# Second expert stage's entry: choice on exponentials, first expert's weights spread by TensorE from the token-major table, two more steps' passes made ahead

## What is computed

```
scores = softmax(x @ gate_w.T)                      # 8 experts, in 4 groups of 2
the 2 groups with the largest scores stay; of their experts the 2 largest are chosen
topk_w = topk_w / topk_w.sum(-1)                    # weights of the two, summing to 1
combine = zeros(T, 8) with the weights at the chosen experts
gate, up = x @ w13[e]  (256 columns each)
out = sum over e of (silu(gate) * up * combine[:, e]) @ w2[e]
```

## Time and profile before

| | |
|---|---|
| median of 3 runs | 1080.58 us |
| profiled execution, time and span | 1081.86 us, 1080.1 us |
| PE busy | 1018.0 us, 94% |
| DVE busy | 817.6 us, 76% |
| ACT busy | 791.2 us, 73% |
| POOL busy | 232.2 us, 21% |
| 16 DMA engines, mean | 176 GB/s |
| chain that ended last | PE 85%; DVE 6%; ACT 3%; POOL 2%; DMA 2%; issue 2% |

### The profile page before, as it was taken

How to read it: one execution, slowest core, us unless ns; L and a number is a source line. 1 busy time by engine, 2 the same in 40 slices (tenths; PEclk the granted TensorE clock), 3 DMA queues, 4 the chain that set the end, 5 groups by cost and what they waited for, 6 DMA issues and landing times.

```text
span 1080.1 us, 20283 instructions
## 1 busy us (share of the span) xinstructions
PE 1018.0 (94%) x5216; PEld 689.6 (64%) x5248; DVE 817.6 (76%) x1867; ACT 791.2 (73%) x1323; POOL 232.2 (21%) x355
## 2 busy tenths in 40 slices
PE   5799999999987799999999999999998998899996
PEld 3233333333345488888888888888875776788884
DVE  8544444444448499999999999999986888589997
ACT  6699999999964587777788777788774443455554
POOL 3777764455452000000000000000014113100000
PEclk9999999999988999999999999999999998899999
DMA  4478786667750587777777777777720000224231
GB/s 137 130 234 261 243 260 229 215 221 235 226 178 1 181 290 238 242 241 242 241 240 241 239 238 243 241 243 243 241 85 25 1 1 1 62 88 136 93 112 40
DMA packets 103422, 190.54 MB, mean 176 GB/s; under 512 B 11980, under 2 KB 56652, under 8 KB 103372
## 3 DMA queue, kind: packets, MB, share of 16 engines
q1 hardware_dynamic: 103380, 190.06, 54.2%
HBM read 154.03 MB, written 35.98 MB: 176 GB/s over the span
## 4 chain that ended last, share of the span: by engine, by line
PE 85%; DVE 6%; ACT 3%; POOL 2%; DMA 2%; issue 2%; SPq 0%; DVEq 0%; POOLq 0%; ACTq 0%
PE bank L1381 27%; PE bank L1394 16%; PE bank L1236 11%; PE bank L1388 8%; PE bank L1217 6%; PE bank L1220 5%; PE bank L1483 2%; PE bank L1247 1%; PE bank L1467 1%; POOL m_norm L831 1%; PE bank L1122 1%; DMA ring<-c_rows 1%; ACT silu_z L1062 1%; DVE xn L1591 1%; PE bank L1486 1%
## 5 line engine op out<-in xcount | busy, mean ns | idle before, releaser
L1381 PE MATMUL bank<-xh,w_parts 128*128 128x512 f32 x896 | 278.3, 392 | 1.6 <-DVEq L1807 1.6
L948 ACT ACTIVATE ring<-bank,minus_bound 128x1024 f32<-128x1024 f32 x256 | 262.6, 1122 | 9.4 <-DVE bank L1688 6.5
L1036 ACT ACTIVATE bank<-bank 128x512 f32<-128x512 f32 x320 | 186.2, 582 | 89.1 <-PE bank L1381 89.1
L1821 DVE TENSOR_TENSOR bank<-bank,ring 128x512 f32<-128x512 f32 x320 | 223.9, 700 | 27.7 <-DMA ring<-c_rows 3.3
L1394 PE MATMUL bank<-hh,w_parts 128*128 128x512 f32 x776 | 239.4, 390 | 0.0
L1813 DVE TENSOR_TENSOR hl<-bank,hh 128x512 fp32r<-128x512 f32 x321 | 218.6, 681 | 0.1
L1030 ACT ACTIVATE hh<-bank 128x512 fp32r<-128x512 f32 x321 | 190.6, 594 | 3.0 <-DVE bank L1821 2.9
L1381 PEld LDWEIGHTS bank<-xh,w_parts 128*128 128x128 f32 x896 | 168.4, 189 | 38.0 <-DVEq L1807 1.8
L1688 DVE TENSOR_TENSOR bank<-bank,corner 128x128 f32<-128x128 f32 x256 | 76.4, 299 | 150.9 <-PE bank L1220 148.5
L1381 PE MATMUL bank<-xl,w_parts 128*128 128x512 f32 x448 | 175.3, 391 | 0.0
L1394 PEld LDWEIGHTS bank<-hh,w_parts 128*128 128x128 f32 x776 | 145.9, 188 | 30.6 <-ACT hh L1030 0.4
(11 more groups left out here) (310 smaller groups left out, 1138.5 us busy)
## 6 DMA issues: line engine op xcount, KB each, us to landing
ring<-c_rows SPq DMA_DIRECT2D x176, 512.0 KB, 4.8
w_parts<-w_pairs SPq DMA_DIRECT2D x160, 128.0 KB, 3.3
w_pairs<-xh SPq DMA_DIRECT2D x16, 768.0 KB, 4.4
q_stack<-q_parts SPq DMA_DIRECT2D x64, 144.0 KB
k_stack<-k_parts SPq DMA_DIRECT2D x192, 48.0 KB
w_pairs<-xl SPq DMA_DIRECT2D x16, 512.0 KB, 3.0
big<-in_w_exp SPq DMA_DIRECT2D x16, 384.0 KB, 4.8
w_ffn_parts<-xl SPq DMA_DIRECT2D x16, 384.0 KB, 3.9
```

The lines of the kernel that those rows point to most:

```text
L948: act.activation(ring[:, c % RING * S:(c % RING + 1) * S], wide[(m + c) % SB][:], ACT.Exp, bias=minus_bound[:]).then_inc(exp_done, 1)
L1036: act.activation(bank(4 + c % ZB), bank(4 + c % ZB), ACT.Silu).then_inc(silu_ready, 1)
L1381: ins = pe.matmul(out_, w[i], x_[j], start=start and k == 0, stop=stop and k == 2, skip_group_check=not start)
L1821: dve.tensor_tensor(bank(4 + c % ZB), bank(4 + c % ZB), cb[u][:, g * GW:(g + 1) * GW], ALU.mult).then_inc(hid_ready, 1)
```

## The change

- The choice works on the shifted logits; the exponentials go to a tile of their own (exp8) and are needed only where the chosen scores are compared. The division by the sum goes, since the weights are divided by their own sum anyway.
- The first expert's weights no longer come by DMA: PE multiplies each tile's column of combine2, read as 128 equal columns (`across`), with the identity, 16 products of 128x128 in plain f32; ACT copies the four banks to cb[0] and raises the semaphores that the DMA raised. The transposes for the other experts' rows follow, each half behind a wait for ACT's copies (cb_loaded), because they use banks 0 to 3 now. ACT makes both row copies. SP loads only expert 1's rows at this place.
- Gate and up of steps 0 and 1 (FT 1, groups 0 and 1) are made ahead, in banks 4 to 7, between FT 0 and the spreading; ACT's two Silus too. In the loop steps 0 and 1 then have no PE work; the products with zeros go, those that open the banks too: each bank is opened by its first high product. The first body of the loop is written out on PE, DVE and ACT.
- DVE's order in a step is now hid n, gated n+4, hl of n-1, in all steps.
- Spare products: 18 for 14 ahead of norm 3, four ahead of each of its later transpositions (L1119), 2 for 12 and 0 for 4 further on.

```diff
@@ -270,6 +270,7 @@
         place = choice(62, 1)
+        exp8 = choice(64, 8).rearrange("p (t e) -> p t e", t=NT)
         earlier = sb("earlier", [P, 4, 4])
@@ -630,8 +631,7 @@
             sp.wait_ge(c_saved, (2 * G + 1) * 16)
-            for u in range(2):
-                load_rows2(u, u)
+            load_rows2(1, 1)
             with sp.Fori(0, NE2 // 2 - 1) as i:
@@ -1074,7 +1074,7 @@
             act.wait_ge(shifted, 1)
-            act.activation(soft[:], soft[:], ACT.Exp).then_inc(exp2_ready, 1)
+            act.activation(exp8, soft[:], ACT.Exp).then_inc(exp2_ready, 1)
             high_x(G - 1)
@@ -1082,20 +1082,40 @@
                 act.activation(first_up[g], bank(2 * (g % 2) + 1), ACT.Copy).then_inc(first_taken, 1)
-            act.wait_ge(c2T_psum, 1)
-            act.activation(c2T[:, 0:S], wide[2][0:NE2, :], ACT.Copy).then_inc(c2T_ready, 1)
-            act.sem_inc(hh2_ready, CREDIT - 1)
+            for c in range(2):
+                ready(act, gate_z, G + c)
+                act.activation(act_out[c], bank(4 + 2 * c), ACT.Silu).then_inc(silu2_ready, 1)
+            for g in range(G):
+                act.wait_ge(c2T_psum, g + 1)
+                ins = act.activation(cb[0][:, g * GW:(g + 1) * GW], bank(g), ACT.Copy)
+                if g % 2:
+                    ins.then_inc(cb_loaded[g // 2], 16)
+            act.sem_inc(hh2_ready, CREDIT)
+
+            def take_c2T(h):
+
+                act.wait_ge(c2T_psum, G + h + 1)
+                act.activation(c2T[:, h * S:(h + 1) * S], wide[h][0:NE2, :], ACT.Copy).then_inc(c2T_ready, 1)
+
+            take_c2T(0)
...
                 n = i * (2 * G) + c
+                if isinstance(i, int) and n < 2:
+                    if n == 1:
+                        high_part(n, c, hid[0], hid2_ready, down2_done, hh2_ready)
+                        take_c2T(1)
+                    return
                 if not last or c < G:
...
-            with act.Fori(0, NE2 - 1) as i:
+            for c in range(2 * G):
+                ffn_step(0, c, False)
+            with act.Fori(1, NE2 - 1) as i:
                 for c in range(2 * G):
@@ -1387,11 +1407,12 @@
-            def down_high(done_step, w, n, ready_high):
+            def down_high(done_step, w, n, ready_high, opens=False):
...
                 ready(pe, ready_high, n)
-                for part in w:
-                    ins = pe.matmul(bank(done_step % G), part, hh[done_step % 2][:], start=False, stop=False, skip_group_check=True)
+                for k, part in enumerate(w):
+                    ins = pe.matmul(bank(done_step % G), part, hh[done_step % 2][:], start=opens and k == 0, stop=False,
+                                    skip_group_check=True)
                 return ins
@@ -1500,10 +1521,11 @@
-            spare(7, 14)
-            norm(3, router_logits2)
-            for opened in (gate_z, up_z, down2_done, low2_used):
-                pe.sem_inc(opened, CREDIT)
+            spare(7, 18)
+            pe.wait_ge(ffn_zero, 1)
+            norm(3, router_logits2, 4)
+            for opened, skipped in ((gate_z, 0), (up_z, 0), (down2_done, 2), (low2_used, 3)):
+                pe.sem_inc(opened, CREDIT + skipped)
             loaded2 = MT_N // CB * 32
@@ -1513,18 +1535,25 @@
                 three(bank(2 * (g % 2) + 1), ffn_parts(0, 1), (xh[:, cols], xl[:, cols]), True).then_inc(up_z, 1)
+            pe.wait_ge(shifted, 1)
+            pe.wait_ge(parts_loaded[CB - 1], loaded2 + 16)
+            for c in range(2):
+                cols = slice(c * GW, (c + 1) * GW)
+                three(bank(4 + 2 * c), ffn_parts(1, 0), (xh[:, cols], xl[:, cols]), True).then_inc(gate_z, 1)
+                three(bank(5 + 2 * c), ffn_parts(1, 1), (xh[:, cols], xl[:, cols]), True).then_inc(up_z, 1)
             pe.wait_ge(first_taken, G)
-            spare(0, 12)
+            spare(0, 2)
             pe.wait_ge(combine2_ready, 1)
-            for t in range(NT):
-                ins = pe.transpose(bank(4 + t // TPG)[0:NE2, t % TPG * P:(t % TPG + 1) * P], combine2[:, t, :], ident[:])
-            ins.then_inc(c2T_psum, 1)
-            spare(0, 4)
-            pe.wait_ge(ffn_zero, 1)
-            pe.wait_ge(c2T_ready, 2)
-            pe.wait_ge(parts_loaded[CB - 1], loaded2 + 16)
-            for g in range(G):
-                pe.matmul(bank(g), ffn_parts(CB - 1, 2)[0], hh[1][:], start=True, stop=False, skip_group_check=True)
+            for g in range(G):
+                for t in range(TPG):
+                    ins = pe.matmul(bank(g)[:, t * P:(t + 1) * P], across(combine2[:, g * TPG + t, 0:1], P), ident[:],
+                                    start=True, stop=True)
+                ins.then_inc(c2T_psum, 1)
+            for h in range(2):
+                pe.wait_ge(cb_loaded[h], MT_N // CB * 16 + 16)
+                for t in range(NT // 2):
+                    ins = pe.transpose(wide[h][0:NE2, t * P:(t + 1) * P], combine2[:, h * (NT // 2) + t, :], ident[:])
+                ins.then_inc(c2T_psum, 1)
@@ -1533,6 +1562,9 @@
                 n, u, g = i * turn_ + c, (c // G + 1) % CB, c % G
+                first = isinstance(i, int) and i == 0
+                if first and c < 2:
+                    return
                 cols = slice(g * GW, (g + 1) * GW)
@@ -1541,13 +1573,18 @@
                     three(bank(4 + 2 * (c % 2)), ffn_parts(u, 0), (xh[:, cols], xl[:, cols]), True).then_inc(gate_z, 1)
-                down_low(low, down2(low), n - 3, hl2_ready).then_inc(low2_used, 1)
+                if not first or c >= 3:
+                    down_low(low, down2(low), n - 3, hl2_ready).then_inc(low2_used, 1)
                 if ahead:
...
                     three(bank(5 + 2 * (c % 2)), ffn_parts(u, 1), (xh[:, cols], xl[:, cols]), True).then_inc(up_z, 1)
-                down_high(high, down2(high), n - 2, hh2_ready).then_inc(down2_done, 1)
-
-            with pe.Fori(0, FT_N // CB - 1) as i:
+                if first and c in (2, 4):
+                    pe.wait_ge(c2T_ready, c // 2)
+                down_high(high, down2(high), n - 2, hh2_ready, first and c < 2 + G).then_inc(down2_done, 1)
+
+            for c in range(turn_):
+                ffn_step(0, c, False)
+            with pe.Fori(1, FT_N // CB - 1) as i:
                 for c in range(turn_):
@@ -1928,12 +1965,10 @@
             dve.tensor_tensor(soft[:], logits, by_row(r_max[:], NE2), ALU.subtract).then_inc(shifted, 1)
-            dve.wait_ge(exp2_ready, 1)
-            link(dve.tensor_reduce(r_sum[:], soft[:], AX.X, ALU.add))
-            link(dve.reciprocal(r_sum[:], r_sum[:]))
-            link(dve.tensor_tensor(soft[:], soft[:], by_row(r_sum[:], NE2), ALU.mult))
             dve.wait_ge(ffn_zero, 1)
+            dve.wait_ge(shifted, 1)
             pairs = soft[:].rearrange("p t (g k) -> p t g k", k=2)
+            exp_pairs = exp8.rearrange("p t (g k) -> p t g k", k=2)
@@ -1950,7 +1985,8 @@
             link(dve.tensor_tensor(won, won, each_token(needed[:], 4), ALU.is_ge))
-            link(dve.tensor_tensor(kept8.rearrange("p t (g k) -> p t g k", k=2), pairs, spread(won, [[4, NT], [1, 4], [0, 2]]), ALU.mult))
+            dve.wait_ge(exp2_ready, 1)
+            link(dve.tensor_tensor(kept8.rearrange("p t (g k) -> p t g k", k=2), exp_pairs, spread(won, [[4, NT], [1, 4], [0, 2]]), ALU.mult))
             for k in range(2):
@@ -1961,14 +1997,12 @@
             link(dve.tensor_tensor(r_sum[:], largest[0], largest[1], ALU.add))
-            link.sign(dve.tensor_tensor(combine2[:], soft[:], picked[0], ALU.mult))
+            link.sign(dve.tensor_tensor(combine2[:], exp8, picked[0], ALU.mult))
             link(dve.reciprocal(r_sum[:], r_sum[:]))
             dve.tensor_tensor(combine2[:], combine2[:], by_row(r_sum[:], NE2), ALU.mult).then_inc(combine2_ready, 1)
-            dve.wait_ge(c2T_psum, 1)
-            dve.tensor_copy(c2T[:, S:2 * S], wide[3][0:NE2, :]).then_inc(c2T_ready, 1)
             dve.sem_inc(gated_ready, CREDIT)
             dve.sem_inc(hid2_ready, CREDIT)
-            dve.sem_inc(hl2_ready, CREDIT)
+            dve.sem_inc(hl2_ready, CREDIT + 1)
             for g in range(G):
@@ -1977,20 +2011,23 @@
                 n, u, g = i * (4 * G) + c, c // (2 * G), c % G
-                if not last or c < 3 * G:
-                    ready(dve, silu2_ready, n + G)
-                    ready(dve, up_z, n + G)
-                    free(dve, hid2_ready, n)
-                    dve.tensor_tensor(gated[(c + G) % 8], act_out[c % 2], bank(5 + 2 * (c % 2)), ALU.mult).then_inc(gated_ready, 1)
                 ready(dve, gated_ready, n)
...
                 dve.tensor_tensor(hid[c % 2], gated[c % 8], cb[u][:, g * GW:(g + 1) * GW], ALU.mult).then_inc(hid2_ready, 1)
-                low_part(n, c, hid[(c - 1) % 2], hh2_ready, low2_used, hl2_ready)
-
-            with dve.Fori(0, NE2 // 2 - 1) as i:
+                if not last or c < 3 * G:
+                    ready(dve, silu2_ready, n + G)
+                    ready(dve, up_z, n + G)
```

(8 more changed lines are left out.)

## The result

The changed kernel takes 1075.88 us (median of 6 runs, 1071.80 to 1079.94); the kernel before 1082.92 us (6 runs, the three known ahead of the prediction among them, 1079.19 to 1085.25). The ratio is 0.9933, 95% interval 0.9911 to 0.9955: faster, by 7.0 us. 1070.6 was forecast, with 1069.0 to 1075.5 as its range. The miss of 5.3 us has two parts of unlike kind: 2.3 us because the kernel before itself measured 1082.92 here and not the 1080.58 from which the sum was subtracted, and 3.0 us because the gain was 7.0 and not 10.0.

The account below looks back on a forecast made before the run. PE was taken to bound the rhythm, so only its start could move: 9.4 us earlier entry plus 0.6 at the end made 10.0, off the 1080.58 median, giving 1070.6 us, range 1069.0 to 1075.5.

Parts of the forecast that it names:

- The last group is normalized at 917.9 as before: Norm on DVE: its end stays at 917.9 us, so last logits come at 920.3 instead of 922.2.
- the entry: From the start of DVE's last normalization to step 5's low product: forecast 27.01 us, against 36.41 before.
- I take it that the clock stays up: PE in the norm: spares cut the wait before 910.84 from 1.9 to 1.0 us, so full clock holds.
- Rival 1: The clock falls in the norm all the same; logits end at about 923, total 1073.3 us; chance 0.11.
- The spreading: PE's 32 identity-product instructions for the first expert's weights: 0.12 us each, 3.8 us, bounds 3.5 to 7.5.
- Rival 2: The clock falls in PE's new 1.4 us wait for ACT's first copy: 1.7 us lost, 1072.3; chance 0.09.
- Rival 4: DVE becomes the bound through a bubble behind low: 1074.2 us, chance 0.11; or slower at 1086.2, chance 0.04.
- The choice: DVE's shorter choice has the table ready at 928.9; worth nothing by itself, since PE arrives at 930.4.
- The end: Loop's end, where DVE leads: the new order starts products behind the last gated one instruction earlier, 0.6 us gained.
- DVE's first weighted product: First expert on DVE: could start at about 933.1 us instead of 943.05.
- The 10.0 us: Total gain forecast: 9.4 us up to step 5's low product plus 0.6 us at the end.

Follow-up runs that it names:

- e1: The changed kernel measured again with nothing edited: median 1075.15 us, ratio 0.9923 to the kernel before.
- e9: The changed kernel measured once more with nothing edited: median 1074.98 us, ratio 0.9917 to the kernel before.
- e3: The changed kernel with POOL's subtractions for xl held back until DVE has normalized all four groups: 1073.34 us, ratio 0.9906 to the kernel before.
- e6: e3's kernel with the softmax's sum, reciprocal and product put back ahead of the choice: 1073.02 us, ratio 0.9904 to the kernel before.
- e10: e3's kernel measured again, POOL held back in the changed kernel: 1073.28 us, ratio 0.9914 to the kernel before.
- e12: e3's kernel without the two spare products ahead of the wait for the weights' table: 1073.95 us, ratio 0.9906 to the kernel before.
- e2: The changed kernel with 14 spare products ahead of the norm and none between its groups: 1078.17 us, ratio 0.9949 to the kernel before.
- e5: e3's kernel with each of the 32 spreading products issued twice: 1074.90 us, ratio 0.9943 to the kernel before.
- e11: e3's kernel with DVE's old order inside a step put back: 1072.61 us, ratio 0.9900 to the kernel before.
- e8: The kernel before, with only POOL's four subtractions held back until DVE has normalized the last group: 1081.92 us, ratio 0.9998 to the kernel before.

## Why the prediction was wrong

**The step that failed**: "The last group is normalized at 917.9 as before". These are DVE and POOL in the kernel before, in rows that I had not put down ahead of the prediction:

```profile
915.89 1.99 DVE L1591 TENSOR_SCALAR xn<-x,mv,rstd 128x128 f32<-128x128 f32 x4 [0.54 <-POOL rstd L677]
...
915.75 1.27 POOL L838 TENSOR_TENSOR xl<-xnT,xh 128x512 fp32r<-128x512 f32 x1
917.91 1.26 POOL L838 TENSOR_TENSOR xl<-xnT,xh 128x512 fp32r<-128x512 f32 x1 [0.89 <-ACT xh L864]
```

The 1.99 us were already a norm under one subtraction; the next one began as it ended, 14.14 us into the stage, since ACT had its group from a PE at half clock. In the changed kernel PE is at full clock, that subtraction begins at 13.52 us (922.92), and the norm is still running. I made PE faster and kept DVE's time, though ACT and POOL stand between them. The last group was done at 15.13 us instead of 14.11. That cost 1.3 us of the entry (e1 and e9 against e3), and behind PE's wait for it came a fall of the clock that none of the seven profiles of the changed kernel with POOL late and the spreading kept (e3 to e6, e10 to e12) has there; where it held for 6.83 us it cost 1.6 more (first profile against e1 and e9). 1.3 and 1.6, less the 0.7 by which e3's entry is better than the forecast, are the 2.25 us (2.94 - 0.69).

**The second step that failed** is the sentence on which the full clock hung: "I take it that the clock stays up, because the idle stretches that remain are no longer than those through which it stayed up". With it the fall behind the norm was put at nothing. PE's wait was 1.08 us, about as long as the 1.0 us at 353.2 that I had taken for safe, and the clock fell. The trace of the kernel before could have said that length doesn't decide: PE stands for 1.56, 1.56 and 2.50 us there (from 360.26, 363.12 and 371.11) with the clock at 1.00 all the while, and for 1.62 us (from 814.32) just ahead of a fall.

I had this very collision in hand: I named POOL's subtraction as the cause of a multiplication of 1.38 us in the choice, and gave it a bound there. I didn't ask the same of the norm. The single instructions of the two groups that each tile query covers say it (duration ns min/median/max), changed kernel and e3:

```profile
L1628 DVE TENSOR_SCALAR xn<-x,mv,rstd x8: 335/344/1361, 919.9 to 924.2; 128x128 f32<-128x128 f32 x8
```

```profile
L1629 DVE TENSOR_SCALAR xn<-x,mv,rstd x8: 338/342/346, 918.5 to 920.9; 128x128 f32<-128x128 f32 x8
```

It is not a slowing by a share. Of the four instructions of the long norm two took 1.220 and 1.361 us, one under each subtraction, and the other two 0.340 and 0.335; each of the long ones ended 0.1 us behind the end of the subtraction over it. In the kernel before, with one subtraction over the norm, it is one of the four (1.216 us, the others 0.33). The Trainium skill ("SBUF — State Buffer", Who interferes with whom) says that VectorE and GpSimd share a pair of ports as an exclusive lock, that a tensor_scalar can take part in it, and that the one issued second blocks until the first is finished. These rows agree with the blocking; the order they can't tell, since the second long instruction and its subtraction start within 0.01 us of each other (922.91 and 922.92). The choice shows the other direction: there a product of DVE with two operands starts at 929.07, the last subtraction of POOL at 929.13, and it is POOL's that is longer, 1.51 instead of 1.27 us, while DVE's keeps its 0.43:

```profile
929.07 0.43 DVE L1983 TENSOR_TENSOR ring<-ring,earlier 128x256 f32<-128x256 f32 x1
...
929.13 1.51 POOL L838 TENSOR_TENSOR xl<-xnT,xh 128x512 fp32r<-128x512 f32 x1 [1.39 <-ACT xh L864]
```

Had I used the page's rule, it would have asked which of POOL's instructions is running when each of DVE's is issued, and that is the question that was missing.

**Rival 1** said that the clock would fall in the norm all the same. It did not: the spares held it up through the three transpositions (without them and the four ahead of the norm, e2 has it at half). It fell behind the last one, by a way that no rival named. The text's own mark, "the forecast falls if the time is above 1072.5: then one of the rivals has set it", was right in its first half only.

**What was right.** The entry without the collision: 16.6, 19.5 and 26.7 us were forecast for the largest logit, the first Silu and the spreading, e3 has 16.39, 19.19 and 26.43. The spreading: 3.57 us by the chain against 3.8, 0.112 us an instruction against 0.12, and wholly on the path (e5). Rival 2: PE's wait for ACT's first copy was 1.29 us in e3 against the 1.4 forecast, and the clock stayed up behind it. Rival 4: the bubble behind the low part is 0.82 - 0.69 = 0.13 us in the loop as at the end, a step on DVE is 948.12 - 946.09 = 2.03 us (forecast 2.02), and PE stays the bound. The choice is worth nothing in the profiled execution of the changed kernel, as forecast, and 0.9 us once the rest is as early as in e3.

**Sizes that were off.** The end gives 0.4 us and not 0.6 (e11). DVE's first weighted product stands at 30.5 us of the stage in e3 and not at 29.3 (933.1): its last wait is for a semaphore that ACT raises only when it has come to its fourth copy (L1093), while the first two copies are done 1.4 us before the product starts; PE doesn't wait for it. The 10.0 us was subtracted from a median of three runs; beside the four sets since then the kernel before stood at 1082.03 to 1083.41, 1.5 to 2.8 us above it, and the range had no room for that. That shift comes from which three runs were taken, not from the mechanism: 2.34 us less would be 1073.54, inside the range, and the two steps above would have been as wrong. The 10.0 us also counts as won the 1.7 us of the second fall of the clock, which e8 doesn't have. Taken as a gain, the kernel with POOL held back gave 10.1 and 8.8 us of the 10.0 forecast, and the changed kernel 7.0, 8.3 and 7.1.

**What stays open.** Why the fall behind the norm lasts 6.83 us in one execution and 3.41 in two others, what makes the clock fall at the stage's start in six of the fourteen profiles, and how often the kernel before has its second fall. Whether the four spares ahead of the last transposition are still of use with POOL late: in e3 PE comes to it 0.7 us after the group is ready, so they lie on the path there, and no run leaves them out. And whether e3's kernel or e12 beats the changed kernel by more than the times can tell: the medians lean to it by 1.0 to 1.8 us, with overlapping intervals.

## What to carry to other kernels

When one engine gets faster, follow what its results release: here PE's clock released ACT, ACT released POOL, and POOL stood on DVE's path two groups later. A duration taken from the trace holds only while the same neighbours run beside it, so look for the shortest row of the same form, and ask what lay over the others (1.12 against 1.99 and 3.01). Work that nobody waits for soon belongs behind the instruction that somebody waits for: one wait on an engine that is off the path gave 1.3 us of the entry (1.7 and 1.8 us by the medians), and the same wait, alone in the kernel before, gave nothing.

## What was not expected of the hardware

Instructions of DVE of 0.34 us took 1.22 and 1.36 us under subtractions of POOL that take 1.27, while POOL's own two in that stretch kept their 1.27; where DVE's product came first by 0.06 us, POOL's subtraction took 1.51. After a wait of 1.08 us on PE, followed by transpositions and products of 8 columns, the granted clock fell to 1.2 GHz in all three profiles of the changed kernel, 1.7 to 2.9 us behind the wait's end; after a wait of 1.29 us in the midst of 512-column products (e3), and after the 1.09 us ahead of the first transposition in the changed kernel itself, it did not. The length of a wait alone, by which I had argued, did not tell the falls apart in these traces.
